# Softmax of the last block: the exponential with its row sums on ScalarE and the division on GpSimd ahead of the transposes, in place of sums by products with a tile of ones

## The reference, cut to what matters

```
h   = layer_norm(x, ln1)                      # 128 x 512
q   = h @ q_w + q_b;  k = ctx @ k_w + k_b;  v = ctx @ v_w + v_b
s   = (q . k over 32 columns of each of 16 heads) / sqrt(32), masked    # 128 x 128 per head
p   = exp(s - max of the row) / (sum of the row)
x   = x + (p @ v, heads side by side) @ cproj_w + cproj_b
x   = x + gelu(layer_norm(x, ln2) @ fc_w + fc_b) @ proj_w + proj_b      # 512 -> 2048 -> 512
```

## Time and profile before

| what | value |
|---|---|
| median of three runs | 4591.57 us (4588.35 to 4592.93) |
| the profiled execution: its own time | 4593.71 us |
| its span in the trace | 4592.0 us |
| mean granted clock of TensorE over the span | 0.959 of full speed |
| TensorE busy | 4193.0 us (91%) |
| VectorE, ScalarE, GpSimd busy | 2349.2, 1503.0, 1421.0 us |
| first full turn of the last block begins | 3099.95 us |
| a full turn of the last block | 194.20 us (3488.46 to 3682.66) |

### The profile page before, as it was taken

One profiled execution on the slowest core, in us unless ns is written; L12 is line 12 of the kernel. 1 busy time (PEld: TensorE's weight loads), 2 busy tenths in 40 slices (PEclk: granted clock), 3 DMA queues, 4 the chain that ended last, 5 costly groups with the idle time before them and its releaser, 6 DMA issues. The chain is left out here.

```text
span 4592.0 us, 78918 instructions
## 1 busy us (share of the span) xinstructions
PE 4193.0 (91%) x30432; PEld 2577.2 (56%) x30432; DVE 2349.2 (51%) x2689; ACT 1503.0 (33%) x2558; POOL 1421.0 (31%) x1181
## 2 busy tenths in 40 slices
PE   7999999995789999999999998689999999999998
PEld 5666666662566666666666666344454444545443
DVE  3656656563466666666666666353343333333330
ACT  2545455453233333333333333212221222212220
POOL 2333333331454444444444443021111111111110
PEclk8999999997899999999999999799999999999999
DMA  3112111113000000000000000030000000000000
GB/s 97 53 63 68 53 65 56 63 44 110 31 15 25 25 24 27 27 34 25 25 25 25 25 25 10 30 122 20 29 1 29 3 27 29 1 29 1 29 10 9
DMA packets 102633, 161.24 MB, mean 35 GB/s; under 512 B 17232, under 2 KB 34768, under 8 KB 101808
## 3 DMA queue, kind: packets, MB, share of 16 engines
q1 hardware_dynamic: 102320, 156.39, 10.1%
HBM read 106.00 MB, written 41.94 MB: 32 GB/s over the span
## 5 line engine op out<-in xcount | busy, mean ns | idle before, releaser
L1375 DVE COPY_PREDICATED b_A<-b_mask,b_pS 128x2048 f32<-128x2048 uint32 x128 | 458.2, 3580 | 234.9 <-PE b_pS L1102 234.5
L1827 PE MATMUL c_pR<-c_proj_w,c_fcT 128*128 128x512 f32 x1024 | 459.5, 597 | 7.5 <-ACTq L1666 3.8
L1761 PE MATMUL c_pR<-c_xT,c_fc_w 128*128 128x512 f32 x1024 | 458.2, 595 | 7.5 <-PEq L1666 2.4
L695 POOL TENSOR_TENSOR a_S<-a_S,a_negmax 128x2048 f32<-128x2048 f32 x64 | 230.9, 3608 | 566.0 <-DVE a_negmax L629 566.0
L1528 POOL TENSOR_TENSOR b_R<-b_R,b_Wh 128x512 f32<-128x512 f32 x192 | 228.5, 1190 | 382.3 <-PE b_pS L1102 381.9
L1102 PE MATMUL b_pS<-b_R,b_kT 32*128 32x128 f32 x7168 | 293.5, 299 | 51.0 <-DVE b_A L1375 21.7
L1978 POOL TENSOR_TENSOR c_S<-c_S,c_negmax 128x1024 f32<-128x1024 f32 x64 | 121.3, 1895 | 702.9 <-DVE c_negmax L1925 702.9
L1951 DVE TENSOR_TENSOR c_res<-c_res,c_pR 128x512 f32<-128x512 f32 x128 | 87.9, 687 | 483.1 <-PE c_pR L1827 449.5
L1761 PEld LDWEIGHTS c_pR<-c_xT,c_fc_w 128*128 128x128 f32 x1024 | 191.4, 190 | 244.5 <-issue 240.8
L1102 PEld LDWEIGHTS b_pS<-b_R,b_kT 32*128 32x128 f32 x7168 | 247.9, 198 | 140.1 <-issue 91.1
L1827 PEld LDWEIGHTS c_pR<-c_proj_w,c_fcT 128*128 128x128 f32 x1024 | 189.7, 190 | 238.4 <-issue 228.0
(11 more groups left out here) (223 smaller groups left out, 8091.9 us busy)
## 6 DMA issues: line engine op xcount, KB each, us to landing
a_c<-ctx SPq DMA_DIRECT2D x16, 512.0 KB, 3.8
a_x<-x SPq DMA_DIRECT2D x16, 512.0 KB, 4.9
a_kexp<-a_kT SPq DMA_DIRECT2D x512, 16.0 KB, 1.8
a_xl<-x SPq DMA_DIRECT2D x32, 256.0 KB, 2.7
a_cl<-ctx SPq DMA_DIRECT2D x32, 256.0 KB, 2.9
mid_x<-a_xl SPq DMA_DIRECT2D x32, 256.0 KB, 2.8
mid_wy<-a_wy SPq DMA_DIRECT2D x32, 256.0 KB, 2.1
b_x1g<-mid_x SPq DMA_DIRECT2D x16, 512.0 KB, 4.1
```

The costliest lines, as they stand in the source:

```text
L695: nc.gpsimd.tensor_tensor(S[n % 2][:, :, :], S[n % 2][:, :, :], negmax[n % 2][:, :].unsqueeze(2).to_broadcast([P, RH, T]), ALU.add)\
L1375: nc.vector.copy_predicated(A[:, :, :].rearrange("p q (n two h) -> p q n two h", two=2, h=h)[:, :, :, 1, :], masks[h][:, :].bitcast(U32).r ...
L1761: mm = nc.tensor.matmul(bank, w[:, c, at * P:at * P + P], src[:, c, :], start=(c == 0), stop=(c == KC - 1))
L1827: mm = nc.tensor.matmul(bank, fcT[part % 2][:, m, g * T:g * T + T], proj_w[:, KC * part + m, :], start=(m == 0), stop=(m == KC - 1))
```

## The change

The list gets an entry `e` per unit, between `s` and `t`. In it ScalarE computes `Exp` in place over `S`, in eight instructions of 128x128, one per square, each with `negmax` as a bias column and with `accum_out`, which leaves the row sums in `wsum` (128 x 8). VectorE takes their reciprocal (`rden`, 128 x 8). GpSimd multiplies all of `S` by it, where it had added `negmax` in entry `s`. TensorE's transposes wait for that product (`weighed`), and ScalarE drains them with `Copy`. Entry `p` on TensorE loses its products with `ones`, and VectorE copies its bank into `attT`. `ones`, its memset and `rec` go. Items and banks of the ring stay as they were. In each engine's order `e0` stands behind R2, `e1` behind v1, `e2` between F5 and v3, `e3` between F6 and F7, `e4` between R5 and t3, `e5` between R6 and R7, `e6` between F8 and F9, `e7` between F10 and F11.

```diff
@@ -1560,8 +1560,8 @@
     VEC0 = vec_column("L3_xattn_ln1_w")
 
 
-    TABLE = """F0 hb F1 cT w1 F2 k0 F3 k1 n1 R0 k2 q0 R1 k3 s0 q1 R2 v0 s1 R3 v1 F4 t0 s2 v2 F5 v3 t1 p0 s3 F6 F7 t2 p1
-               q2 R4 s4 R5 t3 p2 s5 q3 R6 R7 t4 p3 s6 F8 F9 t5 p4 s7 F10 F11 t6 p5 R8 R9 t7 p6 R10 p7 R11
+    TABLE = """F0 hb F1 cT w1 F2 k0 F3 k1 n1 R0 k2 q0 R1 k3 s0 q1 R2 e0 v0 s1 R3 v1 e1 F4 t0 s2 v2 F5 e2 v3 t1 p0 s3 F6 e3 F7 t2 p1
+               q2 R4 s4 R5 e4 t3 p2 s5 q3 R6 e5 R7 t4 p3 s6 F8 e6 F9 t5 p4 s7 F10 e7 F11 t6 p5 R8 R9 t7 p6 R10 p7 R11
                F12 o0 F13 o1 F14 o2 F15 o3 R12 R13 n2 R14 R15""".split()
     LAG = {s: 0 if s[0] in "FRh" else 1 for s in TABLE}
     ITEMS = {}
@@ -1592,14 +1592,14 @@
         vec = sb("vec", [P, dram["vecs"].shape[1] - VEC0])
         rows, ident = sb("rows", [P, 3 * D]), sb("ident", [P, P])
         v_b, cproj_b, proj_b = (rows[:, i * D:i * D + D] for i in range(3))
-        half, ones = sb("half", [P, 1]), sb("ones", [P, HD])
+        half = sb("half", [P, 1])
         x, res, c_xn = sb("x", [P, G, D]), sb("res", [P, G, D]), sb("c_xn", [P, G, D])
         xT1, xT2, cT, kT, qT = sb("xT1", [P, KC, TOK]), sb("xT2", [P, KC, TOK]), sb("cT", [P, KC, TOK]), sb("kT", [P, KC, TOK]), sb("qT", [P, 2, TOK])
         attT = cT
         v_tm = sb("v_tm", [P, G, D])
         S, probsT, fcT = pair("S", [P, UH, T]), pair("probsT", [P, UH, T]), pair("fcT", [P, KC, TOK])
         mask_u8, limit = sb("mask_u8", [P, G * T], U8), sb("limit", [P, G * T])
-        negmax, rec = pair("negmax", [P, UH]), sb("rec", [P, 2 * T])
+        negmax, wsum, rden = pair("negmax", [P, UH]), pair("wsum", [P, UH]), pair("rden", [P, UH])
         bn, mv = sb("bn", [P, G, 6]), sb("mv", [P, G, 2])
         veps, rstd = sb("veps", [P, G]), sb("rstd", [P, G])
         pS = ctx.enter_context(nc.psum_tensor("c_pS", [P, 4, 512], F32))
@@ -1609,14 +1609,15 @@
         emptied = {w: sig("emptied_" + w, [i[1] for i in items].count(w)) for w in ("act", "dve")}
         ring = Ring(items, sig("filled", len(items)), emptied)
         loaded_k, loaded_att, loaded_mlp, held = sig("loaded_k", 0), sig("loaded_att", 0), sig("loaded_mlp", 0), sig("held", 0)
-        consts, ones_set = sig("consts", 0), sig("ones_set", 0)
+        consts = sig("consts", 0)
         c_loaded, mask_loaded = sig("c_loaded", 16), sig("mask_loaded", 16)
         x_loaded, stored = ([sig(n + str(g), 16) for g in range(G)] for n in ("x_loaded", "stored"))
         limit_sign, limit_ready, xb_ready, res_ready = sig("limit_sign", 1), sig("limit_ready", 1), sig("xb_ready", 1), sig("res_ready", G)
-        scored, masked, max_found, shifted, den_inverted = (sig(n, NU) for n in ("scored", "masked", "max_found", "shifted", "den_inverted"))
+        scored, masked, max_found, exp_done, sums_inverted, weighed = (sig(n, NU) for n in ("scored", "masked", "max_found", "exp_done", "sums_inverted",
+                                                                                          "weighed"))
         stats_step, var_ready, rstd_ready, whitened = sig("stats_step", 4 * G), sig("var_ready", 2 * G), sig("rstd_ready", 2 * G), sig("whitened", 2 * G)
         signals = [ring.filled, emptied["act"], emptied["dve"], c_loaded, mask_loaded, limit_sign, limit_ready, xb_ready, res_ready, scored, masked,
-                   max_found, shifted, den_inverted, stats_step, var_ready, rstd_ready, whitened] + x_loaded + stored
+                   max_found, exp_done, sums_inverted, weighed, stats_step, var_ready, rstd_ready, whitened] + x_loaded + stored
         x_v, c_v = dram["x4"].rearrange("b t d -> t b d"), dram["ctx_2048"].rearrange("b t d -> t b d")
         m_v = dram["mask_rows"].rearrange("p b t -> p (b t)")
         block = ctx.enter_context(nc.Block())
@@ -1794,7 +1795,7 @@
                                                   start=True, stop=True)
                     mm.then_inc(*scored.up())
                 elif s[0] == "t":
-                    pe.wait_ge(*shifted(j, n + 1))
+                    pe.wait_ge(*weighed(j, n + 1))
                     for b in range(2):
                         bank = fill(j, s, b)
                         for i in range(4):
@@ -1803,14 +1804,11 @@
                 elif s[0] == "p":
                     c, pair_ = divmod(n, 2)
                     bank = fill(j, s, needs=[("t%d" % n, 1), ("v%d" % (2 * pair_ + 1),)])
-                    pe.wait_ge(ones_set.sem, 1)
-                    for den in range(2):
-                        for b in range(2):
-                            for r in range(P // HD):
-                                head = c * P + r * HD
-                                w = ones[:, :] if den else v_tm[:, 2 * pair_ + b, head:head + HD]
-                                at = (2 * den + b) * T
-                                mm = nc.tensor.matmul(bank[HD * r:HD * r + HD, at:at + T], w, probsT[n % 2][:, 2 * r + b, :], start=True, stop=True)
+                    for b in range(2):
+                        for r in range(P // HD):
+                            head = c * P + r * HD
+                            mm = nc.tensor.matmul(bank[HD * r:HD * r + HD, b * T:b * T + T], v_tm[:, 2 * pair_ + b, head:head + HD],
+                                                  probsT[n % 2][:, 2 * r + b, :], start=True, stop=True)
                     mm.then_inc(*ring.filled.up())
                 elif s[0] == "o":
                     bank = fill(j, s, needs=[("p%d" % (NU - 2 + n // 2),)])
@@ -1850,13 +1848,20 @@
                     ln, dst = ("L3_xattn_ln1_", xT1) if s == "n1" else ("L3_xattn_ln2_", xT2)
                     for c in range(KC):
                         drain(j, dst[:, c, :], s, c, bias=col(ln + "b", c), scale=col(ln + "w", c))
+                elif s[0] == "e":
+                    act.wait_ge(*max_found(j, n + 1))
+                    act.wait_ge(*(sums_inverted(j, n - 1) if n >= 2 else sums_inverted.before(j, n + NU - 1)))
+                    for i in range(UH):
+                        ins = nc.scalar.activation(S[n % 2][:, i, :], S[n % 2][:, i, :], ACT.Exp, bias=negmax[n % 2][:, i:i + 1],
+                                                   accum_out=wsum[n % 2][:, i:i + 1])
+                    ins.then_inc(*exp_done.up())
                 elif s[0] == "t":
                     if n >= 2:
                         act.wait_ge(*full(j, "p%d" % (n - 2)))
                     elif (j + -1).exists():
                         act.wait_ge(*full(j + -1, "p%d" % (n + NU - 2)))
                     for b in range(2):
-                        drain(j, probsT[n % 2][:, 4 * b:4 * b + 4, :].rearrange("p h t -> p (h t)"), s, b, func=ACT.Exp)
+                        drain(j, probsT[n % 2][:, 4 * b:4 * b + 4, :].rearrange("p h t -> p (h t)"), s, b, func=ACT.Copy)
                 elif s[0] == "F":
                     part = n // KC
                     if part >= 2:
@@ -1923,15 +1928,17 @@
                         .then_inc(*masked.up())
                     dve.wait_ge(*masked(j, n + 1))
                     nc.vector.tensor_reduce(negmax[n % 2][:, :], S[n % 2][:, :, :], AX.X, ALU.max, negate=True).then_inc(*max_found.up())
+                elif s[0] == "e":
+                    dve.wait_ge(*exp_done(j, n + 1))
+                    if n >= 2:
+                        dve.wait_ge(*weighed(j, n - 1))
+                    else:
+                        dve.wait_ge(*weighed.before(j, n + NU - 1))
+                    nc.vector.reciprocal(rden[n % 2][:, :], wsum[n % 2][:, :]).then_inc(*sums_inverted.up())
                 elif s[0] == "p":
                     c, pair_ = divmod(n, 2)
-                    if n:
-                        dve.wait_ge(*out(j, "p%d" % (n - 1)))
                     bank = take(dve, j, s)
-                    nc.vector.reciprocal(rec[:, :], bank[:, 2 * T:4 * T]).then_inc(*den_inverted.up())
-                    dve.wait_ge(*den_inverted(j, n + 1))
-                    nc.vector.tensor_tensor(attT[:, c, 2 * pair_ * T:2 * pair_ * T + 2 * T], bank[:, 0:2 * T], rec[:, :], ALU.mult)\
-                        .then_inc(*emptied["dve"].up())
+                    nc.vector.tensor_copy(attT[:, c, 2 * pair_ * T:2 * pair_ * T + 2 * T], bank[:, 0:2 * T]).then_inc(*emptied["dve"].up())
                 elif s[0] == "o":
                     dve.wait_ge(*xb_ready(j, 1))
                     bank = take(dve, j, s)
@@ -1954,7 +1961,6 @@
 
         @block.gpsimd
         def _(pool):
-            nc.gpsimd.memset(ones[:, :], 1.0).then_inc(*ones_set.up())
             pool.wait_ge(consts.sem, 1)
             pool.wait_ge(loaded_att.sem, loaded_att.seen)
 
@@ -1973,10 +1979,10 @@
                         deviation(j, 0, g)
                     pool.wait_ge(*whitened(j, G))
                     nc.gpsimd.tensor_tensor(x[:, :, :], x[:, :, :], cproj_b.unsqueeze(1).to_broadcast([P, G, D]), ALU.add).then_inc(*xb_ready.up())
-                elif s[0] == "s":
-                    pool.wait_ge(*max_found(j, n + 1))
```

(6 more changed lines are left out.)

## The result

The changed kernel takes 4635.7 us in the median of six runs (4626.48 to 4643.8) against 4592.66 us for the kernel before in six (4588.35 to 4596.82). The ratio is 1.0093, 95% interval 1.0082 to 1.0104: 43 us slower. The forecast said 4616 us within 4593 to 4650. The profiled execution of the changed kernel is the fastest of its six, 4626.48 us with a span of 4624.8, so its span is 32.8 us over that of before. The median of all six is 43 us over; where the 10 us between the two figures lie is taken up under "The whole".

What follows compares the result with a forecast made beforehand. TensorE was taken to set the pace. Per turn 6.63 us of stalls against 3.68 saved gave +2.95, +20.7 in seven, plus 4 ahead of the loop: +24.7, forecast 4616 us, range 4593 to 4650.

Steps and rivals of the forecast that it cites:

- q2: TensorE waits here for a bank whose Gelu drain stands behind a unit's exponentials: stall E - 0.76 = 2.24 us per turn.
- F10: TensorE waits here for the bank of F9, drained behind a unit's exponentials: stall E - 1.42 = 1.58 us per turn.
- R8: TensorE waits here for the bank of F11, drained behind a unit's exponentials: stall E - 0.76 = 2.24 us per turn.
- F6: TensorE waits here for the bank of v3, drained by VectorE, which waits for ScalarE: stall 0.57 us per turn.
- e0: List entry with a unit's exponentials, behind R2: drains behind waiting VectorE are due a step or more later, 0 charged.
- e5: List entry with a unit's exponentials, between R6 and R7: drains behind waiting VectorE due a step or more later, 0 charged.
- break-even: In a full turn, three stalls of together 3E - 2.94 equal the 3.68 us saved at E = 2.2 us.
- E: Time a unit's eight Exp with accumulator reads hold ScalarE: put at 3.0 us, ends 2.4 and 4.7.
- clock case: Rival: stalls at TensorE bring stretches at 1.2 GHz, +24 us on top, 4640 us; chance 7 in 100.
- cheap case: Rival: ScalarE's accumulator reads are hidden, E = 2.4 us, +6 us in all, 4598 us; chance 13 in 100.
- faster case: Rival: short activations on ScalarE overlap, E about 1.6 us, -12.7 us in the loop, 4578 us; chance 12 in 100.
- dear case: Rival: nothing overlaps on ScalarE, E = 4.7 us, +77 us, 4669 us; chance 8 in 100.

Runs made afterwards that it cites:

- e2: The kernel before with only the products with the tile of ones left out: 4567.51 us, ratio 0.9941.
- e1: The changed kernel with four list entries moved: three exponential entries ahead of the Gelu drains they stood behind, one behind v3; 4571.49 us, ratio 0.9957 to the kernel before.
- e3: The changed kernel with the products with ones put back on TensorE, their result not read: 4653.6 us, ratio 1.0133 to the kernel before.
- e6: The changed kernel with one entry moved, the exponentials between F6 and F7 put ahead of F6: 4620.13 us, ratio 1.0059 to the kernel before.
- e7: The changed kernel with one entry moved, the exponentials between F5 and v3 put behind v3: 4631.23 us, ratio 1.0085 to the kernel before.
- e4: The changed kernel with four Exp of 128x256 per unit in place of eight of 128x128: 4593.13 us, ratio 1.0 to the kernel before.
- e8: The changed kernel with Tanh in place of Gelu in the MLP, so no table loads between: 4576.48 us, ratio 0.9962 to the kernel before.

## Why the prediction was right

**The sum, term by term.** Per full turn:

| term | forecast | measured | where |
|---|---|---|---|
| products with ones gone | -3.68 | -3.50 | e2 |
| q2 | +2.24 | +2.48 | changed kernel |
| F10 | +1.58 | +1.81 | changed kernel |
| R8 | +2.24 | +2.48 | changed kernel |
| F6 | +0.57 | +0.71 | changed kernel |
| sum | +2.95 | +3.98 (the turn: +3.96) | |

The measured delays are start to start: from p to q2 and to R8 3.05 us (3583.14 to 3586.19, 3631.16 to 3634.21) where 0.575 would do, from s7 to F10 2.47 and from s3 to F6 1.37 where 0.66 would. They are some 0.08 us more than the idle times: without a wait a step starts 0.07 us before the one ahead of it has ended (p is 0.64 us long and the next step starts 0.575 after it), and behind a wait it doesn't.

**The mechanism** was right in the steps of the sum: which four places, in what order of size, by whose release, the number of loads, the 0 charged at the transposes and at e0, e1, e4 and e5, and the break-even. e1 shows it by taking the four away, e3 by the halved return of the ones, e6 and e7 by one place each. The clock was not in the sum.

**What was off is a size.** E was put at 3.0 us and is 3.20. I had the spacing of the 128-wide Exp at 0.36; it is 0.387. The 0.2 us count at four places and so are 0.8 of the missing 1.03 us a turn; 0.18 is the ones, and 0.05 is left over the four places together. How 0.387 comes about can be read off the rows: one Exp lasts 0.388 us and the accumulator's read 0.187, and each overlaps its neighbour by about 0.094, 0.388 + 0.187 - 2 x 0.094 = 0.387. The forecast's own rows gave nearly that: at 512 elements 0.686 + 0.203 come every 0.68 us, so the two overlaps are 0.21 together, and with the 0.39 that the forecast put for the length of the last Exp and 0.20 for its read, 0.59 - 0.21 = 0.38. Instead it added 0.03 us for an Exp in place from SBUF to the length, and only 0.01 to the spacing.

**Ahead of the loop** I put +4: 3.1, and 0.9 that might be between 0 and 3. From the first scores to the first product of the first turn it is 87.94 us (3010.65 to 3098.59) where the kernel before has 82.15 (3017.80 to 3099.95), +5.8:

```profile
3010.65 0.73 PE L1794 MATMUL c_pS<-c_kT,c_qT 32*128 32x128 f32 x16
...
3098.59 1.98 PE L1762 MATMUL c_pR<-c_xT,c_fc_w 128*128 128x512 f32 x4 [1.56 <-ACT c_xT L1836]
```

```profile
3017.80 0.73 PE L1793 MATMUL c_pS<-c_kT,c_qT 32*128 32x128 f32 x16
```

(the second fence is the kernel before). That it is E that counts here too follows from e4, where it is 82.23 us (3011.93 to 3094.16), and from e8, which has E as it was and no table loads and takes 87.92 (3019.59 to 3107.51). It is not the clock: the mean granted clock over the stretch is 0.90 in the changed kernel and in e4 alike (0.96 in the kernel before).

**The whole.** 7 x 3.96 = 27.7, 5.8 ahead of the loop, 4 spells at 1.2 GHz of 1.7 us = 6.8, together +40.3; but the profiled execution reached its first scores 7.2 us earlier (3010.65 for 3017.80), in blocks that the change leaves alone. That makes 33.1 of the 32.8 measured. Of the way from the forecast's 24.7 us to the median's 43 the loop is 7.0, the start 1.8 and the clock, as far as the trace shows it, 6.8: the spells, which I had held for a rival of 7 in 100 at +24, in truth come on top, with a part of that. The 2.7 us that are left no trace shows.

The direction and the four places were earned. That the time lies well inside the range owes something to its width: 4635.7 is what the prediction gives for E = 3.6 (4635) and is near its clock case (4640), and neither is what happened. With E at 3.20 its own sum gives +24.7 + 7 x 0.8 + 4 x 0.2 = +31.1, an estimate; the clock, which the sum had at nothing, is 6.8 of the 12 left.

**Rivals.** The cheap case and the faster case needed E of 2.4 and 1.6; both fall to E = 3.20. The dear case needed spacings of 0.59 with no overlap; there is overlap. The longer table change (a drain of about 1.38 us to each load, the Trainium skill, page "ScalarE: Activation LUTs", section "What ACT_TABLE_LOAD costs") doesn't show here either: the drain of F6 ends at 3579.64, the load at 3579.65 lasts 1.28 and the Exp starts at 3580.95. The advice of the Trainium skill, page "VectorE: DVE Perf Modes", section on the TRN2 errata, to keep operations at 512 elements or more points the right way: going from 128 to 256 elements (e4) brings a unit from 3.20 to 2.10 us. Its figure of 350 cycles, an estimate of 0.29 us, is of a copy; an Exp with bias and sum comes every 0.387 us here.

## What to carry to other kernels

Work moved to an engine that is idle two thirds of the time is paid for by where it stands in that engine's order: ask which drain is queued behind it, which bank that drain frees, and how many microseconds the bottleneck has left before it needs the bank. Here two table loads and eight small activations between two drains gave 5.8 us where there were 3.3 to 4.0 to spare (5.8 less the delays of 2.48 and 1.81); the same exponentials ahead of the first of the two drains, with four fewer table loads in a turn, cost 0.14 us of a turn and turned 0.9% slower into 0.4% faster. That order has no room left, so it should be timed again after any change near it. Count a table change with the work that brings it, and place that work next to other work of the same table.

## What the runs showed of the hardware that was not expected

- Exp of 128x128 from SBUF with a bias column and a sum: 0.388 us long, one every 0.387 us, with a read of the accumulator of 0.187 us between. Of 128x256: one every 0.49 to 0.51.
- A wait of TensorE of 1.74 to 2.40 us in otherwise unbroken work was followed by a spell at 1.2 GHz in some turns and not in others, at 1.7 us each (5.23 for 3.54 us); waits of 1.3 us or less never were (21 in e4's loop at 1.29 or less, and those of 1.24 ahead of n2 in every kernel).
